# A fused two-layer perceiver block: masks, series and projections moved to where engines wait

## The chip, the cores and the metric

The kernel runs on one core of one Trainium2 chip. The metric is the device time of one execution of the whole program, in microseconds (us), lower is better. TensorE is called PE, VectorE DVE, ScalarE ACT, GpSimd POOL, and the queue of SyncE, from which the loads are issued, SP.

## The reference

Six residual sublayers work on x, 8 batches of 64 tokens of 512 numbers. Each takes the layer norm of x and adds its result to x.

```python
x = x + _L0_xattn_ref(_layernorm(x), ctx_2048, itok, ...)   # windowed latent attention over 9 context rows
x = x + _L0_attn_ref(_layernorm(x), ...)                    # differential attention
x = x + _L0_ffn_ref(_layernorm(x), w_gate_up, w_proj)       # ternary weights, silu(gate) * up, rms norm, projection
x = x + _L1_xattn_ref(_layernorm(x), ctx_2048, decay, W_in, b_in, W_out, b_out, gamma, beta)
x = x + _L1_attn_ref(_layernorm(x), ...)                    # int8 projections, rotary attention
x = x + _L1_ffn_ref(_layernorm(x), ...)                     # Hadamard transforms, 2048 hidden
...
good = (k_ids <= qs) & (k_ids >= qs - LOOKBACK)             # L0_xattn: 9 rows of 1601 per token, by its id
...
s = K * s + xt                                              # L1_xattn: x = kv W_in + b_in, K = sigmoid(decay)
summary = jnp.mean(states @ W_out.T + b_out, axis=1)        # one row per batch
```

Only the mean over the 1601 states of the fourth sublayer counts, so the kernel works with two weighted sums of the context rows per batch: the plain mean, and the sum weighted by a decay series of 1601 numbers.

## The kernel before, in words

One program in raw engine code: each engine has its own list of instructions, in the order in which the functions are called at the end of the file, and semaphores tie them. Nothing is scheduled; the order written is the order run. Most products are taken in three matmuls of fp32r parts (`mm3`, L41 to L43: high by high, low by high, high by low). A high part is a cast on ACT (`split_high`, L153, for weights), a low part a subtraction on POOL (`split_low`, L157) or DVE.

**Start of WindowAttention.** DVE makes the decay series as one scan of 1601 steps in one partition (`vector_series`, L324), sums it (`vector_total`, L329), turns the token ids into row numbers for the gathers (`ids`, L954 to L967), and then does the layer norm of x (L190 to L208, with PE turning xn and ACT taking the high part). PE spreads the series over partitions by 13 matmuls of one column (`tensor_columns`, L349 and L350). After the layer norm DVE takes the low parts of two weights (L1014), copies the group ids (L1016), and makes the masks of the windows (`group_masks`, `key_masks`: L974 to L997; `empty_windows`: L1003 to L1007). PE then makes the query latents `wa_qc` from W_dq (24 matmuls).

**Units of keys.** Four gathers (`wa_win`) bring 9 context rows for each of 128 tokens. They are worked off in 12 units u of three rows: PE turns (`turn`, L1173), ACT takes the high part (L855), DVE the low part (`keys_low`, L1029), PE compresses (`compress`, 12 matmuls), DVE copies to `wa_kst` (L1039), PE makes the rope keys (`rope_keys`, L1191). POOL rotates them (`rotate`, L770 to L775), PE turns the result (`rope_turn`, L1200), ACT copies it (`rope_out`, L847).

**Pairs of heads.** For 8 pairs i PE makes queries (L41 to L43, L1245), rope queries and `wa_qa`. ACT copies `wa_qn` high (L886), the sums of the pair before (`rotated`, four copies, L877), the rope keys, and then casts the weights of the next pair (L153), of which POOL takes the low parts (L157). PE begins pair i+1 when these are there.

**Rounds of attention.** 18 rounds of scores, softmax and context follow, with matmuls of the context sums among them until round 12.

**Seam to the ternary FFN and its rounds.** DiffAttention ends with x += (L1634); SP then issues loads, among them `ContextSummary.sync` (bias and two 1 MB weights); DVE, PE and ACT do the layer norm. PE makes 16 hidden tiles f, each a gate and an up product of 8 f16 matmuls (L2087). In the last two rounds it also does `tensor_state` (L410, L411: four groups of matmuls with 8 columns) and `tensor_summary` (L418, L419), both in one piece. ACT casts the projection weights `ff_wp` (L2030) after the last round; PE projects (L2101, L2102).

**Int8Attention.** ACT copies, takes exponentials and, between them, casts the first two weights of the last FFN (`ffn.high`, L2679); POOL takes their low parts (L2649). DVE scales y (L2369).

## Time and profile before

| what | value |
|---|---|
| median of 3 runs | 940.71 us (937.42 to 946.45) |
| profiled execution, its own time | 947.03 us |
| its span | 945.1 us |
| PE busy | 845.2 us (89%) |
| DVE busy | 617.8 us (65%) |
| ACT busy | 479.0 us (51%) |
| POOL busy | 167.9 us (18%) |
| mean granted clock of PE | 0.931 of full speed |

The span runs from the first to the last instruction; 1.9 us lie around it. The profiled execution is 6.3 us, or 0.7%, above the median of the three timed runs. Times in rows are counted from the start of the span.

### The profile page before, as it was taken

What the parts mean: (1) busy time and instruction counts of PE and PEld (TensorE: products, weight loads), DVE (VectorE), ACT (ScalarE), POOL (GpSimd) and SP (SyncE); (2) the same over time, 40 slices, a digit from 0 to 9 for tenths busy, and PEclk for the clock granted to TensorE, in tenths of its full rate; (3) what the DMA queues carried; (4) which work ended last, traced back from release to release, by engine and by line L of the source; (5) the groups of instructions that cost most, each with busy time, mean ns of one, the idle gap of its engine ahead of it and who ended that gap; (6) DMA issues with size and microseconds to landing.
All of it is one profiled execution on the core that took longest, in us unless ns stands there. A gap on an engine that the chain in (4) does not pass through costs nothing.

```text
span 945.1 us, 13986 instructions
## 1 busy us (share of the span) xinstructions
PE 845.2 (89%) x5323; PEld 638.2 (68%) x5323; DVE 617.8 (65%) x1056; ACT 479.0 (51%) x798; POOL 167.9 (18%) x168
## 2 busy tenths in 40 slices
PE   4899899999899798999999987998967666999997
PEld 4797555677778576887887874454743445888885
DVE  7654677567466658999999985433587877434233
ACT  2466675223275488777878643432335443434331
POOL 2044541000145410000000001331031112111112
PEclk9999999999589889999999999998988766999999
DMA  8633465761113544334443005004042610221201
GB/s 281 221 131 109 147 198 209 293 229 52 57 56 100 179 139 156 103 102 136 131 156 112 23 2 181 0 0 171 29 141 90 246 46 1 67 66 46 68 1 44
DMA packets 49628, 106.77 MB, mean 113 GB/s; under 512 B 6484, under 2 KB 25868, under 8 KB 45982
## 3 DMA queue, kind: packets, MB, share of 16 engines
q1 hardware_dynamic: 48670, 95.31, 30.3%
q0 software_dynamic: 896, 10.62, 2.9%
q8 instruction: 41, 0.67, 0.3%
q14 instruction: 21, 0.17, 0.1%
HBM read 100.67 MB, written 5.24 MB: 112 GB/s over the span
## 4 chain that ended last, share of the span: by engine, by line
PE 75%; DVE 12%; ACT 6%; issue 2%; POOL 1%; SPq 1%; DMA 1%; ACTq 0%; DVEq 0%; POOLq 0%
PE banks L41 15%; PE banks L43 14%; PE banks L42 14%; PE banks L2087 6%; PE banks L359 2%; PE banks L1339 2%; PE banks L2101 2%; PE banks L1309 2%; PE banks L2102 2%; PE banks L1710 2%; PE banks L1901 1%; PE banks L1312 1%; PE banks L1173 1%; PE banks L1191 1%; ACT tw_wide L1868 1%
## 5 line engine op out<-in xcount | busy, mean ns | idle before, releaser
L157 POOL TENSOR_TENSOR w_low<-w_raw,w_high 128x256 fp32r<-128x256 f32 (+2 forms) x44 | 58.2, 1332 | 175.0 <-ACT w_high L153 174.9
L153 ACT CAST w_high<-w_raw 128x1024 fp32r<-128x1024 f32 (+2 forms) x74 | 56.9, 780 | 23.8 <-PE banks L43 18.2
L41 PE MATMUL banks<-da_xT_high,w_high 128*128 128x512 f32 x128 | 52.6, 411 | 1.4 <-DVE da_xT_low L208 1.4
L41 PE MATMUL banks<-hf_xhh,w_high 128*128 128x512 f32 (+1 forms) x136 | 51.8, 381 | 0.4 <-DVE hf_xhl L2754 0.3
L43 PE MATMUL banks<-hf_xhh,w_low 128*128 128x512 f32 (+1 forms) x136 | 51.9, 382 | 0.0
L42 PE MATMUL banks<-hf_xhl,w_high 128*128 128x512 f32 (+1 forms) x136 | 51.8, 381 | 0.0
L2087 PE MATMUL banks<-ff_xT_high,tw_guT 128*128 128x512 f16 x128 | 49.8, 389 | 1.4 <-DVE ff_xT_low L208 1.4
L43 PE MATMUL banks<-da_xT_high,w_low 128*128 128x512 f32 x128 | 50.9, 398 | 0.0
L42 PE MATMUL banks<-da_xT_low,w_high 128*128 128x512 f32 x128 | 50.7, 396 | 0.0
L2087 PE MATMUL banks<-ff_xT_low,tw_guT 128*128 128x512 f16 x128 | 49.7, 388 | 0.0
L2670 POOL TENSOR_TENSOR hf_hl<-hf_h,hf_hh 128x512 fp32r<-128x512 f32 x16 | 24.3, 1519 | 124.7 <-ACT hf_hh L2726 124.7
L2734 DVE TENSOR_TENSOR hf_downW_l<-dw_w,hf_downW_h 128x512 fp32r<-128x512 f32 x16 | 11.2, 697 | 50.7 <-ACT hf_downW_h L2686 50.7
L1989 POOL MEMSET ff_acc<- 128x512 f32 x1 | 0.5, 530 | 239.9 <-DVE x_res L1634 239.9
L1578 DVE TENSOR_TENSOR w_low<-w_raw,w_high 128x1024 fp32r<-128x1024 f32 x28 | 33.7, 1224 | 6.6 <-ACT w_high L153 5.9
L41 PE MATMUL banks<-w_high,da_xT_high 128*128 128x256 f32 x128 | 37.1, 290 | 0.0
L43 PE MATMUL banks<-w_high,da_xT_low 128*128 128x256 f32 x128 | 36.2, 283 | 0.0
L42 PE MATMUL banks<-w_low,da_xT_high 128*128 128x256 f32 x128 | 36.1, 282 | 0.0
L2783 DVE TENSOR_TENSOR hf_downH_l<-banks,hf_downH_h 128x512 fp32r<-128x512 f32 x16 | 11.1, 692 | 35.0 <-ACT hf_downH_h L2722 35.0
L1868 ACT CAST tw_wide<-banks 128x1024 bf16<-128x1024 f32 x24 | 24.5, 1020 | 18.5 <-PE banks L1901 18.5
L912 ACT COPY wa_cn<-banks 72x512 f32<-72x512 f32 x16 | 9.3, 582 | 48.2 <-PE banks L1320 48.2
L2049 DVE TENSOR_TENSOR ff_e<-ff_e,banks 128x512 f32<-128x512 f32 x16 | 11.0, 688 | 34.1 <-PE banks L2087 34.1
L2716 ACT ACTIVATE hf_silu<-banks,hf_scales 128x512 f32<-128x512 f32 x16 | 11.0, 690 | 43.2 <-PE banks L43 43.2
(433 smaller groups left out, 2523.4 us busy)
## 6 DMA issues: line engine op xcount, KB each, us to landing
cs_rows<-in_ctx SPq DMA_DIRECT2D x24, 1024.0 KB, 5.0
tw_raw<-in_L_ffn_w_gate_up SPq DMA_DIRECT2D x16, 512.0 KB, 4.4
hf_raw<-in_L_ffn_W_up SPq DMA_DIRECT2D x16, 512.0 KB, 3.6
w_raw<-in_L_xattn_W_o SPq DMA_DIRECT2D x8, 512.0 KB
w_raw<-in_L_attn_Wq SPq DMA_DIRECT2D x8, 512.0 KB
w_raw<-in_L_attn_Wk SPq DMA_DIRECT2D x8, 512.0 KB
w_raw<-in_L_attn_Wv SPq DMA_DIRECT2D x8, 512.0 KB
w_raw<-in_L_attn_Wo SPq DMA_DIRECT2D x8, 512.0 KB
```

The source lines that it names most:

```text
L41: nc.tensor.matmul(out, a[0], b[0], start=start, stop=False)
L42: nc.tensor.matmul(out, a[0], b[1], start=False, stop=False)
L43: return nc.tensor.matmul(out, a[1], b[0], start=False, stop=stop)
L153: self.nc.scalar.copy(self.wh[k][:, 0:cols], self.raw[k][:, 0:cols]).then_inc(self.split_hi[k], 1)
L157: self.nc.gpsimd.tensor_tensor(self.wl[k][:, 0:cols], self.raw[k][:, 0:cols], self.wh[k][:, 0:cols].bitcast(F32), ALU.subtract).then_inc(s ...
L359: ins = nc.tensor.matmul(c.bank[32 * r:32 * r + 32, bank, :], self.col[:, k * self.R4 + r, :], self.rows[k][:, r, :], start=(k == 0), stop ...
L1309: nc.tensor.matmul(out[a], queries(self.qa, 8 * g), keys(self.kvcT[:, g // 16, g % 16, :, :]), start=True, stop=False)
L1339: ins = nc.tensor.matmul(c.bank[:, 6 + r % 2, q * P:(q + 1) * P], self.cn[(r - 2) % 3][:, q, :], self.pt[r % 2][:, q, :], start=True, stop ...
L1578: v.tensor_tensor(c.wl[k][:, :], c.raw[k][:, :], c.wh[k][:, :].bitcast(F32), ALU.subtract).then_inc(c.split_lo[k], 1)
L1868: self.c.nc.scalar.copy(self.wide[s % self.DEEP][:, :].rearrange("p (a n) -> p a n", a=2), self.c.bank[:, bank:bank + 2, :]).then_inc(self ...
L2087: ins = nc.tensor.matmul(c.bank[:, 2 * k + n, :], w.guT[:, j, bass.ds(i * 2 * P + k * P + n * F0, P)], part[:, j, :], start=(j == 0 and pa ...
L2670: g.tensor_tensor(self.hp[1][t % 2][:, :], self.h[t % 2][:, :], self.hp[0][t % 2][:, :].bitcast(F32), ALU.subtract).then_inc(self.hl_ok, 1)
```

## The change

What it does, by places:

- **Start.** The ids and their base load first on SP, before x. `ids` runs first on DVE, then the series; the total of the series, the ids of groups and all masks leave the start. The low part of W_dq is taken inside the layer norm (`ahead`), ahead of `xT_low`. The layer norm turns over four banks in place of two. PE's 13 matmuls of the series are gone: SP writes the series to DRAM and reads it back as columns (`sync_columns`), DVE scales them.
- **Units.** The six pieces lie after the copy to `wa_kst` of units 0 to 5 on DVE. The group ids' matmul is after unit 1 on PE. `rope_turn(6)` moves from the last unit to behind it, into one row with 7 and 8; banks of two rope turns change.
- **Pairs.** ACT casts the next weights ahead of `rotated`. POOL's first three `low` stand behind both halves of the last rotation.
- **Seam and FFN.** `ContextSummary.sync` is issued when the ternary weights are done, before DiffAttention ends. `tensor_state` is cut into four: two right after the first x +=, two in tiles 1 and 2; `tensor_summary` into four in tiles 4 to 7; its bias is added on DVE. The first gate and up products are done in halves of 256 tokens, the first when two of four `xT_low` are there. Four of eight rounds are written out, the rest stay a loop. ACT casts `ff_wp` 0 and 1 after its first round. `load_second` of the down weights is issued once the summary is done.
- **Int8Attention.** Both `ffn.high` come between the first exponentials and `turned(3)`.

```diff
@@ LayerNorm.vector_rest
                                     ALU.subtract, ALU.mult).then_inc(c.ln_xn, 1)
+        if ahead:
+            ahead(dve)
         if self.transposed:
@@ ContextSums
+    def sync_columns(self, sp):
+        sp.wait_ge(self.geo_ok, 1)
+        sp.dma_start(self.series, self.geo).then_inc(self.col_done, 16)
+        sp.wait_ge(self.col_done, 16)
+        sp.dma_start(self.col_in[:, 0:self.R], ...).then_inc(self.col_done, 16)
+            sp.dma_start(self.col_in[0:self.rest, self.R:self.R + 1], ...).then_inc(self.col_done, 16)
-    def tensor_columns(self, pe, at):
@@ ContextSummary
+    def tensor_state(self, pe, j):
+        if j == 0:
+            pe.wait_ge(cs.mean_ready, B)
...
+            pe.wait_ge(self.in_, 16 * 4)
+    def tensor_summary(self, pe, k):
+        if k == 0:
+            pe.wait_ge(self.cs.s_out, 1)
@@ WindowAttention.gpsimd
-            rotate(m, 0)
-            if m == M - 1:
-                low(0, 1)
-                low(1, 1)
-            rotate(m, 1)
+            for a in range(2):
+                rotate(m, a)
+        low(0, 1)
+        low(1, 1)
+        c.split_low(pool, 2, f[2] + 3, 2 * LAT)
@@ WindowAttention.scalar
+            if i < PAIRS - 1:
+                act.wait_ge(self.qr_done, i + 1)
+                high(0, i + 1)
+                high(1, i + 1)
             if i:
                 rotated(i - 1)
             if i in (1, 2, 3):
                 rope_out(8 + i)
-            if i < PAIRS - 1:
-                act.wait_ge(self.qr_done, i + 1)
-                high(0, i + 1)
-                high(1, i + 1)
@@ WindowAttention.vector, after the copy to wa_kst of unit u
+            if u == 0:
+                self.segments(dve, ch)
+            if u == 1:
+                self.cs.vector_total(dve, ch)
+            if u == 2:
+                self.group_masks(dve, ch)
+            if u == 3:
+                ch.wait()
+                self.cs.vector_columns(dve)
+                self.key_masks(dve, ch)
+            if u == 4:
+                self.key_offsets(dve, ch)
+            if u == 5:
+                self.empty_windows(dve, ch)
@@ WindowAttention.tensor
-            if u == self.UNITS - 1:
-                rope_turn(u - 5)
...
-        rope_turn(7)
-        rope_turn(8)
+            if u == 1:
+                pe.wait_ge(self.seg_f, 1)
+                nc.tensor.matmul(c.bank[:, 7, 0:self.G], self.rep[:, :], self.seg8f[:, 1, :], ...).then_inc(self.g_done, 1)
+        for u in (6, 7, 8):
+            rope_turn(u)
@@ TernaryFFN
+        round_(0, True)
+        projection(0)
+        projection(1)
...
+        def among(f):
+            if f in (1, 2):
+                self.cy.tensor_state(pe, f + 1)
+            if 4 <= f < 4 + C:
+                self.cy.tensor_summary(pe, f - 4)
+        early, late = slice(0, 2 * P), slice(2 * P, N)
+        pe.wait_ge(c.ln_lo, M * self.ln.t + 2)
+        for n in range(2):
+            product(0, n, early)
+        pe.wait_ge(c.ln_lo, M * self.ln.t + M)
@@ Int8Attention.scalar
         exponentials(0)
+        for t in range(2):
+            self.ffn.high(act, t)
         turned(3)
         probabilities(0)
         exponentials(1)
-        self.ffn.high(act, 0)
@@ build
+                window.sync_ids(sp)
                 sp.dma_start(core.ident[:, :], dram["ident"]).then_inc(core.const_in, 16)
...
+                sp.wait_ge(ternary.q_ok, ternary.STEPS)
+                ffn0.cy.sync(sp)
                 after_diff(sp)
...
+                pe.wait_ge(diff.y_add, 1)
+                for j in range(2):
+                    ffn0.cy.tensor_state(pe, j)
                 after_diff(pe)
```

On DVE, from the series to the first low part of the query latents, this stood before (`wa_segf`: ids as numbers, `wa_idx`: rows to gather, `wa_g`, `wa_vb`, `wa_vt`: masks):

```order
L324 SCALAR_TENSOR_TENSOR wa_kvcT<-cs_decay,cs_ones 1x1601
L329 TENSOR_REDUCE cs_tot<-wa_kvcT 1x1
L963 CAST wa_idx<-wa_segf 128x4
L190 BN_STATS ln_stats<-x_res 128x6 x4
L208 TENSOR_TENSOR wa_xT_low<-banks,wa_xT_high 128x4x128 x4
L1014 TENSOR_TENSOR w_low<-w_raw,w_high 128x1024
L1016 COPY wa_g<-banks 128x64
L992 TENSOR_TENSOR wa_vb<-wa_jrow,wa_g 128x576
L997 TENSOR_SCALAR wa_vb<-wa_vt 128x576
L1023 TENSOR_TENSOR wa_qcl<-banks,wa_qch 128x512
L1003 CAST wa_segs<-wa_segb 128x512
```

And this stands there now, on the same engine, up to the first units (rows between are left out in both):

```order
L980 CAST wa_idx<-wa_segf 128x4
L337 SCALAR_TENSOR_TENSOR wa_krT<-cs_decay,cs_ones 1x1601
L190 BN_STATS ln_stats<-x_res 128x6 x4
L1037 TENSOR_TENSOR w_low<-w_raw,w_high 128x1024
L210 TENSOR_TENSOR wa_xT_low<-banks,wa_xT_high 128x4x128 x4
L1037 TENSOR_TENSOR w_low<-w_raw,w_high 128x512
L1045 TENSOR_TENSOR wa_qcl<-banks,wa_qch 128x512 x2
L1049 TENSOR_TENSOR wa_cT_even_l<-banks,wa_cT_even_h 128x4x128 x3
L1059 COPY wa_kst<-banks 128x384
L985 CAST wa_seg8f<-wa_seg 8x64
L342 TENSOR_REDUCE cs_tot<-wa_krT 1x1
```

The low part of W_dq is ahead of `xT_low`, and nothing but the other weight's low part lies between `xT_low` and the query latents. The masks are among the units.

On ACT, in pair 1 of the heads, before (`wa_qnh`: queries high, `wa_qr`: rope queries, `w_high0` to `w_high2`: weights of the next pair):

```order
L886 CAST wa_qnh1<-banks 128x512
L877 COPY wa_qr<-wa_t10 64x256 x4
L847 COPY wa_krT<-banks 64x16x8 x3
L153 CAST w_high0<-w_raw 128x384
L153 CAST w_high1<-w_raw 128x256
L898 COPY wa_qa<-banks 128x512
L153 CAST w_high2<-w_raw 128x256
```

The same pair now:

```order
L904 CAST wa_qnh1<-banks 128x512
L153 CAST w_high0<-w_raw 128x384
L153 CAST w_high1<-w_raw 128x256
L895 COPY wa_qr<-wa_t10 64x256 x4
L866 COPY wa_krT<-banks 64x16x8 x3
L916 COPY wa_qa<-banks 128x512
L153 CAST w_high2<-w_raw 128x256
```

The two casts have passed the four copies of `wa_qr` and the rope keys.

On PE, between the last product of DiffAttention and the first hidden tile, the layer norm's turns stood alone before; now:

```order
L43 MATMUL banks<-w_high3,da_ol1 128x512
L418 MATMUL banks<-cs_mu,cy_wT0 128x8 x4
L419 MATMUL banks<-cs_tot,cy_bias0 128x8
L418 MATMUL banks<-cs_mu,cy_wT0 128x8 x4
L419 MATMUL banks<-cs_tot,cy_bias0 128x8
L243 MATMUL banks<-ident,ff_xn 128x128 x16
L2116 MATMUL banks<-ff_xT_high,tw_guT 128x256
L2116 MATMUL banks<-ff_xT_low,tw_guT 128x256
```

Two of the four groups of `tensor_state` stand at the seam, and the first products are halves.

## Rows read from the trace of the kernel before

**Rows 1.** The page: busy time of engines, and the chain that ended last.

```profile
PE 845.2 (89%) x5323; PEld 638.2 (68%) x5323; DVE 617.8 (65%) x1056; ACT 479.0 (51%) x798; POOL 167.9 (18%) x168
...
PE 75%; DVE 12%; ACT 6%; issue 2%; POOL 1%; SPq 1%; DMA 1%; ACTq 0%; DVEq 0%; POOLq 0%
```

**Rows 2.** Timeline, 0 to 36: start, duration, engine, line; in brackets idle before, releaser.

```profile
6.91 1.81 DVE L329 TENSOR_REDUCE cs_tot<-wa_kvcT 1x1 f32<-1x1601 f32 x1
...
11.08 2.45 DVE L190 BATCH_NORM_STATS2 ln_stats<-x_res 128x6 f32<-128x512 f32 x4
...
15.24 1.11 PE L241 MATMUL banks<-ident,wa_xn 128*128 128x128 f32 x4 [0.81 <-DVE wa_xn L203]
...
20.44 0.69 DVE L208 TENSOR_TENSOR wa_xT_low<-banks,wa_xT_high 128x512 fp32r<-128x512 f32 x1 [0.16 <-ACT wa_xT_high L231]
...
23.15 0.77 PE L41 MATMUL banks<-wa_xT_high,w_high 128*128 128x512 f32 x1 [3.36 <-DVE wa_g L1016]
...
31.89 0.43 DVE L1003 CAST wa_segs<-wa_segb 128x512 f32<-128x512 int32 x1 [2.67 <-DMA wa_cs<-in_q_sin]
...
35.96 0.44 PE L41 MATMUL banks<-wa_cT_even_h,w_high 128*128 128x384 f32 x1 [0.54 <-DVE wa_cT_even_l L1029]
```

**Rows 3.** Timeline: a low part of the units on DVE, the last unit on PE.

```profile
40.94 1.29 DVE L1029 TENSOR_TENSOR wa_cT_even_l<-banks,wa_cT_even_h 128x512 fp32r<-128x512 f32 x2 [2.04 <-ACT wa_cT_even_h L855]
...
83.87 0.52 PE L1200 MATMUL banks<-ident,wa_kr 128*64 128x128 f32 x3 [1.43 <-POOL wa_kr L775]
```

**Rows 4.** Waits of PE, whole span: total us, times, longest; then timeline, 99 to 105.

```profile
PE banks L41 <- POOL w_low L157: 4.4, 4, 2.3
...
99.65 2.60 ACT L877 COPY wa_qr<-wa_t 64x256 f32<-64x256 f32 x4 [0.21 <-POOL wa_t L806]
...
104.32 0.50 PE L41 MATMUL banks<-wa_qch,w_high 128*128 128x512 f32 x1 [2.30 <-POOL w_low L157]
```

**Rows 5.** Windows: length, busy of PE, PEld, DVE, ACT, POOL, granted clock, DMA, GB/s.

```profile
104.00:108.00 4.00, 3.68 (x13) 2.10 (x13) 0.83 (x1) 0.64 (x2) 2.89 (x4) 0.67 0.30 86
160.00:234.00 74.00, 73.06 (x602) 52.57 (x601) 48.55 (x133) 24.24 (x47) 0.73 (x1) 1.00 0.58 211
234.00:262.00 28.00, 23.44 (x112) 20.61 (x112) 15.33 (x39) 9.26 (x15) 3.08 (x2) 0.52 0.14 48
635.00:641.10 6.10, 6.10 (x20) 3.57 (x21) 0.47 (x2) 0.00 (x0) 0.00 (x0) 0.50 0.00 0
651.00:655.20 4.20, 3.53 (x9) 2.82 (x10) 2.75 (x4) 1.14 (x3) 1.27 (x1) 0.59 0.97 348
```

**Rows 6.** Timeline, the seam to the ternary FFN on PE.

```profile
576.06 3.34 PE L241 MATMUL banks<-ident,ff_xn 128*128 128x128 f32 x16 [3.38 <-DVE ff_xn L203]
...
580.79 0.39 PE L2087 MATMUL banks<-ff_xT_high,tw_guT 128*128 128x512 f16 x1 [1.40 <-DVE ff_xT_low L208]
```

**Rows 7.** Timeline, 630 to 652, PE: state, summary, first projection.

```profile
630.88 0.95 PE L410 MATMUL banks<-cs_mu,cy_wT 128*128 128x8 f32 x8
...
637.19 0.61 PE L2087 MATMUL banks<-ff_xT_high,tw_guT 128*128 128x512 f16 x1
...
642.73 3.60 PE L418 MATMUL banks<-cy_wT,cy_stateT 128*8 128x512 f32 x8
...
651.67 0.80 PE L2101 MATMUL banks<-ff_wp,ff_hh 128*128 128x512 f32 x1 [2.55 <-ACT ff_wp L2030]
```

**Rows 8.** Timeline, Int8Attention: an ACT copy, POOL's low part, DVE's scaling twice.

```profile
748.35 0.69 ACT L2232 COPY w_raw<-banks 128x640 f32<-128x640 f32 x1 [2.66 <-PE banks L2452]
...
752.68 2.42 POOL L2649 TENSOR_TENSOR w_low<-hf_raw,w_high 128x1024 fp32r<-128x1024 f32 x1 [22.64 <-ACT w_high L2679]
...
753.56 1.82 DVE L2369 TENSOR_SCALAR ia_y<-ia_y,ia_y_scale 128x512 f32<-128x512 f32 x1
...
756.75 1.51 PE L2498 MATMUL banks<-ia_v,ia_aT 64*64 64x33 f32 x64 [2.98 <-ACT ia_aT L2245]
...
769.07 0.48 DVE L2369 TENSOR_SCALAR ia_y<-ia_y,ia_y_scale 128x512 f32<-128x512 f32 x1
```

217 lines of the change are left out of this document (113 added, 104 removed).

## The prediction, made before the changed kernel was run

> **What bounds the kernel now.** The page comes first, for the busy shares and the chain that ended last. PE is busy for 89% of the span and carries 75% of that chain; DVE has 12% of it, ACT 6% [rows 1]. So the work on PE is the floor, and this change takes hardly any of it away: time can come from the places where PE stands idle, and from stretches in which PE works at a low granted clock. I looked for both. The waits of PE by what ended them and the timeline of PE, with what DVE, ACT and POOL did just before, give the idle places; the windows give the clock. The reader is to see in them that most of the waits are short, that the longest lie where a helper engine has a queue of other work in front of the one thing PE needs, and that two clock dips follow late stretches of narrow or interrupted PE work. The attention rounds, the longest part, are full at clock 1.00 over 160 to 234 [rows 5] and are not touched. The sum is made against the profiled execution's own time, 947.03 us; the median of the runs is 6.3 us below it, and I take that off at the end.
>
> **Start: 5.9 us (4.2 to 7.3).** The first compress of PE starts at 35.96. On DVE the series' sum, 1.81, stands ahead of the layer norm's statistics at 11.08 [rows 2]; it leaves for the units, so with the ids still ahead they start at about 9.3, and the first turn at 13.4 in place of 15.24. From first turn to last low part the layer norm takes 5.9 here (15.24 to 20.44 + 0.69 = 21.13) [rows 2], while the larger one at the seam takes 4.7 (576.06 to 580.79) [rows 6]; with four banks I take 4.7 here as well: ready at 18.1. PE's product then started at 23.15, behind the weight's low part and the copy of the group ids, which PE waited 3.36 for [rows 2]. Both are gone from there, so it starts at about 18.5: 4.65 us. After it, the mask of empty windows waited 2.67 on DVE for a load, with the second low part of the query latents behind it [rows 2]; I take half, 1.3, since PE had half of that stretch filled. The lower end is that the constants land no earlier and the statistics stay at 11.08 (less 1.7), the upper that the whole 2.67 comes back. The gathers now follow the ids directly and PE wants them only after the queries; SP's trip of the series through DRAM is wanted by nobody before the context sums.
>
> **Units: 0.2 us (-1.0 to 1.0).** PE's wait of 1.43 before the rope turn of unit 6 goes with the move of `rope_turn(6)`, but the turn itself comes later in one row with two others; I count 0.7. The group ids' matmul on PE costs up to 0.4. The masks now lie on DVE between low parts of keys. The idle slot there is 2.04 a unit [rows 3], and the one piece that has a row, the sum of the series, is 1.81 [rows 2], so each piece about fills its slot; I take 0.1 for what spills over. If each of six spilled 0.2, the term would be -1.0. If the slots covered all and the turn were hidden, it would be 1.0.
>
> There is a row that speaks against this placing. A scaling of `ia_y` on DVE took 1.82 with POOL's low part running beside it from 752.68, and 0.48 without such company [rows 8]. POOL rotates rope keys beside the units, and the key masks of unit 3 on DVE fall on that. The Trainium skill, GPSIMD Engine Reference, section 1 (Specifications), says that the engine's SBUF interfaces are shared with VectorE, with contention when DVE works in a 2-port mode or reads two SBUF inputs. The trace agrees for the scaling (0.48 against 1.82); by it, the masks, some of which read two tiles, would spill more. By the rows, I let it stand in the lower bound, because the rotation covers one unit out of six.
>
> **Pairs: 4.6 us (1.5 to 6.5).** PE waits four times for POOL's low part of a weight, 4.4 in all, the longest 2.30 at 104.32 [rows 4]. The cast on ACT that POOL needs stands behind four copies of 2.60 together, which start at 99.65 [rows 4]; now it stands ahead of them. After that longest wait the granted clock over 104 to 108 is 0.67 [rows 5]; its 4 us did the work of 2.7, so 1.3 more is lost there. 5.7 is there to be had. A quarter of the waits, 1.1, I keep back, since ACT is nearly full in these pairs and now brings the rotated queries and `wa_qa` 0.5 to 1 us later, which PE wants too: 4.6. POOL's first three low parts behind the last rotation have the rest of that unit as cover. At the low end ACT becomes the bound and returns only the clock and a little; at the top nothing is given back and the lost share of the clock is larger.
>
> **Seam: 0.9 us (-0.9 to 1.7).** PE stood idle 3.38 before the layer norm's turns and 1.40 before the first gate product [rows 6]. Two of four state groups, some 2.6 us by half of the 6.3 below less the slow clock, go into the first gap, nearly covered; the half product starts when two low parts of four are there, so most of the 1.40 can be used. I count 0.9, since the extra matmuls of halved products and the turns that now start behind state groups cost some. The low bound is that the 2 MB of weights land late: SP issues them some 10 us before they are wanted.
>
> **State out of the last rounds: 3.7 us (3.0 to 4.0).** The four groups run from 630.88 to 637.19, 6.3 us with no product beside them [rows 7]. Two remain in PE's stream, in tiles 1 and 2, at 1.3 each: 2.6.
>
> **Half clock behind it: 2.0 us (0 to 2.0).** From 635 to 641.1 the granted clock is 0.50, with PE busy for all of the 6.10 [rows 5]. What ran just before was the row of matmuls with 8 columns. About 2 of the 3 us lost there fall on ordinary products, which I expect at full clock once the narrow ones are spread out. That is a reading, not a proof, so 0 is the lower end. The Trainium skill, TensorE: Matmul & The Clock Gate, Part 1 (The HAM clock gate), says that the clock is set by how busy PE has been recently; the trace agrees only in part, with 0.50 over a stretch in which PE's records have no gap, and by the page alone I would count 0 here.
>
> **Summary: 0.4 us (-0.8 to 1.4).** Its eight wide matmuls are 3.60 of PE at 642.73 [rows 7] and stay; the bias matmuls go (about 1.4), and three more entries and exits among the products cost up to 1.
>
> **Wait for `ff_wp`: 2.55 us (2.0 to 2.6),** at 651.67, on ACT's cast [rows 7]. The cast moves to after the first round, 60 us ahead. Next late would be POOL's part, wanted only after the following tile: covered. **Half clock around it: 1.5 us (0 to 1.7).** From 651 to 655.2 it is 0.59 [rows 5], a loss of 1.7; without the wait ahead I take 1.5 back.
>
> **Heads of Int8Attention: 2.1 us (0 to 3.0).** ACT stands idle 2.66 before 748.35, and both of `ffn.high` go there. POOL's low part, which waits for them [rows 8], then runs earlier and no longer beside DVE's scaling at 753.56: 1.82 - 0.48 = 1.34. The cast no longer stands in the way of the next outputs, about 0.8. PE's idle 2.98 before 756.75 [rows 8] is the end of that chain and can take both.
>
> **Sum.** 5.9 + 0.2 + 4.6 + 0.9 + 3.7 + 2.0 + 0.4 + 2.55 + 1.5 + 2.1 = 23.85. From 947.03 that leaves 923.2, and 6.3 less is 916.9. I predict 917 us, 2.5% faster; with the smaller bounds partly met, 912 to 922.
>
> **The rivals.**
>
> *New waits take the place of the old (927, 922 to 932).* ACT, moved first, becomes late with `rotated` and `wa_qa`, and the pairs give 1.5 (3.1 less); both clock dips stay, because something else than the narrow matmuls and the wait makes them (3.5 less); the masks spill by 1.0 (1.2 less); the heads wait for PE's turns instead (2.1 less). Together 9.9 less. For it: ACT's load in the pairs, and the 0.50 with PE fully busy. Against it: each wait removed has a named cause with another piece of work ahead of it in the queue, and these are gone.
>
> *Loads are late (933, 930 to 938).* The change then does not do at the start and seam what it says: the ids' small load holds up the constants, the gathers or weights land after PE wants them, and the start gives 1.5 rather than 5.9, the seam -0.9. That is 6.2 beyond the case above. Against it: from the ids to the first turn of context rows there are some 18 us.
>
> *More (909).* The terms reach towards their upper ends: start 1.4, pairs 1.9, seam 0.8, summary 1.0, heads 0.9, units 0.8, and a little more.
>
> *Slower (953).* The clock, not the waits: over 234 to 262 the granted clock is 0.52, against 1.00 over the 74 us before [rows 5]. If the changed order ahead of the attention rounds left PE at the half level for their whole first stretch, 160 to 234, the cost, by the row at 0.52, would be 0.48 for each us spent in it. 75 us more of such a dip cost 36, and 917 becomes 953. It decides from 50 us of new half clock on, which eat the whole gain. Against it: nothing in that stage is changed.
>
> **How the numbers follow.** Chances: forecast 0.56, new waits 0.27, more 0.08, late loads 0.05, slower 0.04. The likeliest gives 917. From 908 to 931 the range takes in the forecast, the smaller gain and nearly all of the larger, and leaves out late loads, the slower case and the tails, under 2 in 10. One per cent, down to 931.3, is about what a measurement of this kernel can tell from no change. Faster by over 1%: the first three cases less a small tail, 0.90; within 1%: 0.06; slower: 0.04.
>
> **What the profile after would show.** The span near 921. First compress near 30. The waits of PE on POOL's low part of a weight together below 1.5, and no new waits of a us on ACT's copies in the pairs. No PE wait of a us in the last unit; idle slots of DVE in units 0 to 5 gone, with the unit's period the same. A granted clock near 1 where the rounds of the ternary FFN end and at its first projection, with no wait for `ff_wp`. The scaling of `ia_y` in the first head at 0.48. I am wrong if the two clock dips are still there, if ACT's copies stand as the enders of PE's waits, or if a product of the start waits for a load.

## The result and the profile after

The changed kernel takes 912.79 us in the median of 4 runs (910.99 to 913.76), the kernel before beside it 939.07 (935.98 to 946.45). The ratio is 0.9714, 95% interval 0.9678 to 0.9749. I had predicted 917 with 908 to 931 as the range. The profiled execution took 912.06 us, with a span of 910.0. Ratios leave out executions over 1.5% longer than the fastest of their kernel: none in these eight, three of 56 of the kernel before in the experiments.

The page of the changed kernel, busy time of the engines and the chain that ended last:

```profile
PE 815.7 (90%) x5298; PEld 621.0 (68%) x5311; DVE 614.0 (67%) x1056; ACT 480.3 (53%) x798; POOL 171.6 (19%) x168
...
PE 78%; DVE 14%; ACT 5%; issue 2%; DMA 0%; POOL 0%; SPq 0%; ACTq 0%; DVEq 0%
```

PE is busy for 29.5 us less than in [rows 1], although hardly any of its work went: many matmuls that ran at half clock there run at full clock here (mean granted clock 0.950 against 0.931). A part of that belongs to the one execution that [rows 1] show, as the first experiment says.

The timelines of DVE and PE at the start, to be read against [rows 2]: start, duration, engine, line; in brackets the idle time before, and what ended it.

```profile
9.66 2.43 DVE L190 BATCH_NORM_STATS2 ln_stats<-x_res 128x6 f32<-128x512 f32 x4
```

```profile
13.90 3.65 PE L243 MATMUL banks<-ident,wa_xn 128*128 128x128 f32 x16 [13.90 <-DVE wa_xn L203]
...
18.95 0.50 PE L41 MATMUL banks<-wa_xT_high,w_high 128*128 128x512 f32 x1 [1.40 <-DVE wa_xT_low L210]
...
23.88 0.39 PE L41 MATMUL banks<-wa_xT_high,w_high 128*128 128x512 f32 x1
...
28.64 0.44 PE L41 MATMUL banks<-wa_cT_even_h,w_high 128*128 128x384 f32 x1 [0.54 <-DVE wa_cT_even_l L1049]
```

The statistics start 1.4 earlier, the product of the query latents at 18.95 in place of 23.15, and the first compress at 28.64 in place of 35.96. Of these 7.3 us, 1.7 lie inside the product: it takes 4.93 from its first L41 to its last, where before it took 6.66 (23.15 to 29.81), the first matmul of it 0.50 against the 0.77 of [rows 2]. The next seven took 0.63 each before and 0.39 to 0.40 now. The windows show a granted clock of 1.00 over this product in both, so it is from the matmuls' own times that I call those of 0.63 half clock: matmuls of this shape take 0.63 in the changed kernel at 238 to 242, where the granted clock is 0.50.

The waits of PE in the stretch of the pairs, 80 to 160, in the changed kernel:

```profile
PE banks L41 <- issue: 1.0, 1, 1.0
PE banks L1341 <- DVE wa_qa L1109: 0.6, 1, 0.6
PE banks L41 <- ACT wa_kr_odd L859: 0.5, 1, 0.5
PE banks L41 <- DVE wa_t L1097: 0.4, 1, 0.4
```

The wait on POOL's low parts, 4.4 in [rows 4], is not there any more. What came in its place are 0.6 us ahead of the first scores and 0.4 ahead of another product. ACT is busy for 46.17 of the 60.60 us of that stretch, and it never ended a wait of PE on a pair's weights.

The seam on PE, against [rows 6]:

```profile
549.81 1.03 PE L418 MATMUL banks<-cs_mu,cy_wT 128*128 128x8 f32 x8 [0.29 <-DMA cy_wT<-in_L_xattn_W_out]
550.77 0.38 PE L419 MATMUL banks<-cs_tot,cy_bias 1*128 1x8 f32 x2
551.09 1.06 PE L418 MATMUL banks<-cs_mu,cy_wT 128*128 128x8 f32 x8
...
552.90 3.15 PE L243 MATMUL banks<-ident,ff_xn 128*128 128x128 f32 x16 [0.44 <-DVE ff_xn L203]
555.84 0.42 PE L2116 MATMUL banks<-ff_xT_high,tw_guT 128*128 128x256 f16 x1
```

Two groups of the state fill the gap of 3.38 down to 0.44, and the gap of 1.40 ahead of the first gate product is gone. The weights had landed but for 0.29.

Where [rows 7] had a wait of 2.55, the first projection follows directly, and the windows show no dip there (length, busy time of PE, PEld, DVE, ACT, POOL, granted clock, share of DMA, GB/s):

```profile
618.11 0.59 PE L2159 MATMUL banks<-ff_wp,ff_hh 128*128 128x512 f32 x1
```

```profile
614.00:618.00 4.00, 4.00 (x20) 1.83 (x19) 1.29 (x2) 1.33 (x4) 0.96 (x1) 1.00 0.00 0
618.00:622.00 4.00, 4.00 (x19) 3.01 (x16) 2.35 (x3) 2.06 (x4) 2.68 (x2) 1.00 0.52 172
622.00:626.00 4.00, 4.00 (x22) 3.35 (x22) 0.16 (x1) 1.42 (x3) 0.07 (x1) 1.00 0.99 363
```

### The profile page after: what moved, and what is told of

Same layout as the page of the kernel before. It is cut to its first block, busy times and chain, and to the rows that moved or that the text cites. A ratio compares the mean times of both kernels' runs of the same rounds, so it can differ in the third digit from the quotient of the medians.

```text
span 910.0 us, 13910 instructions
## 1 busy us (share of the span) xinstructions
PE 815.7 (90%) x5298; PEld 621.0 (68%) x5311; DVE 614.0 (67%) x1056; ACT 480.3 (53%) x798; POOL 171.6 (19%) x168
## 4 chain that ended last, share of the span: by engine, by line
PE 78%; DVE 14%; ACT 5%; issue 2%; DMA 0%; POOL 0%; SPq 0%; ACTq 0%; DVEq 0%
PE banks L41 16%; PE banks L43 15%; PE banks L42 15%; PE banks L2131 6%; PE banks L364 2%; PE banks L2159 2%; PE banks L1341 2%; PE banks L2160 2%; PE banks L1742 2%; PE banks L1371 1%; PE banks L1202 1%; PE banks L1344 1%; PE banks L1933 1%; ACT tw_wide L1900 1%; PE banks L243 1%
## 5 line engine op out<-in xcount | busy, mean ns | idle before, releaser
L41 PE MATMUL banks<-da_xT_high,w_high 128*128 128x512 f32 x128 | 52.5, 410 | 1.4 <-DVE da_xT_low L210 1.4
L41 PE MATMUL banks<-hf_xhh,w_high 128*128 128x512 f32 (+1 forms) x136 | 52.3, 385 | 0.2 <-DVE hf_xhl L2812 0.2
L2131 PE MATMUL banks<-ff_xT_high,tw_guT 128*128 128x512 f16 x120 | 45.5, 380 | 0.0
L2131 PE MATMUL banks<-ff_xT_low,tw_guT 128*128 128x512 f16 x120 | 45.5, 379 | 0.0
L41 PE MATMUL banks<-w_high,da_xT_high 128*128 128x256 f32 x128 | 37.1, 290 | 0.0
```

Source lines behind the costliest of these rows:

```text
L41: nc.tensor.matmul(out, a[0], b[0], start=start, stop=False)
L2131: ins = nc.tensor.matmul(c.bank[:, 2 * k + n, :], w.guT[:, j, bass.ds(i * 2 * P + k * P + n * F0, P)], part[:, j, :], start=(j == 0 and pa ...
```

## The experiments

Twelve experiments follow. The kernel before, run beside them, took 938.1 to 939.7 in the median.

To read them I cut each trace at the same eight places on PE and take the lengths between: the first compress, the first product of the pairs, the first scores, the first product of the output behind the attention rounds, the first gate product, the first projection, the first turn of Int8Attention, the first product of the last FFN, and the end of the span. "Before" is the profile that the prediction had, "again" the second one of the same kernel; the last column is the median of the timed runs. One stretch can differ by 1 us or more between two profiles of the same code in it, by where the clock is low.

| kernel | start | units | pairs | rounds | to gate | tiles | projection to Int8 | Int8 | rest | span | median |
|---|---|---|---|---|---|---|---|---|---|---|---|
| before | 35.96 | 53.17 | 68.19 | 109.08 | 314.39 | 70.88 | 64.60 | 79.58 | 149.25 | 945.1 | 939.07 |
| again | 35.61 | 53.16 | 67.05 | 100.90 | 315.17 | 70.83 | 64.60 | 79.63 | 149.15 | 936.1 | 938.43 |
| changed | 28.64 | 52.65 | 60.59 | 100.86 | 313.10 | 62.27 | 63.46 | 78.22 | 150.21 | 910.0 | 912.79 |
| ACT's order undone | 28.13 | 52.64 | 66.78 | 101.29 | 312.99 | 62.41 | 63.42 | 77.66 | 149.18 | 914.5 | 916.81 |
| state at the end | 30.03 | 52.65 | 60.91 | 100.82 | 313.04 | 66.09 | 63.10 | 78.22 | 150.24 | 915.1 | 916.24 |
| casts late | 27.77 | 52.64 | 60.54 | 101.22 | 313.79 | 64.74 | 64.40 | 77.86 | 149.54 | 912.5 | 915.01 |
| state in a row | 29.91 | 52.64 | 60.56 | 100.81 | 314.25 | 66.11 | 63.46 | 78.34 | 149.32 | 915.4 | 915.30 |
| `ffn.high` undone | 28.02 | 52.63 | 61.04 | 101.17 | 313.22 | 61.83 | 63.29 | 79.87 | 149.23 | 910.3 | 913.06 |
| masks in front | 41.64 | 52.32 | 61.57 | 100.90 | 314.64 | 61.77 | 63.34 | 78.13 | 149.69 | 924.0 | 924.55 |
| two banks | 32.27 | 52.64 | 61.58 | 101.09 | 314.19 | 61.77 | 63.59 | 78.64 | 149.53 | 915.3 | 914.57 |
| ACT's order alone | 36.02 | 53.20 | 60.51 | 100.76 | 314.32 | 72.49 | 63.03 | 79.70 | 149.27 | 929.3 | 931.41 |
| masks in a lump | 28.32 | 61.36 | 61.54 | 100.60 | 313.17 | 62.50 | 63.41 | 77.19 | 149.21 | 917.3 | 920.24 |
| fillers in five waits | 28.18 | 52.65 | 60.72 | 101.02 | 314.08 | 61.77 | 63.21 | 74.88 | 149.79 | 906.3 | 911.94 |
| fillers in Int8 | 30.17 | 52.64 | 60.62 | 100.61 | 314.90 | 61.77 | 63.39 | 74.29 | 148.01 | 906.4 | 911.21 |

**The kernel before, profiled again.** No edit.

> The kernel before, profiled once more. In its first profile the granted clock is 0.50 to 0.59 from 234 to 264, in the attention rounds behind the last context sum; the changed kernel has 1.00 in the same rounds, which makes 8.7 us of the 35 us between the two profiled spans. Theory A (the dip is a state that some executions have, not a part of the change): the new profile, or some of the timed runs, shows no such dip; span 935 to 940 with a mean clock near 0.95, and over all runs the time falls as the mean clock rises. Theory B (the dip belongs to the program of before, and the change removed it): the dip starts again within a few us of 234, span 944 to 947, mean clock 0.93.

Theory A. The span is 936.1, the rounds 100.90. The windows of the second profile and those of the first, in the same part of the attention rounds (columns as above):

```profile
236.00:242.00 6.00, 6.00 (x55) 5.63 (x55) 5.46 (x17) 2.07 (x4) 0.20 (x1) 1.00 0.30 105
```

```profile
242.00:250.00 8.00, 8.00 (x40) 7.26 (x40) 3.70 (x11) 1.47 (x3) 0.00 (x0) 0.50 0.01 2
250.00:262.00 12.00, 7.44 (x31) 6.09 (x31) 5.79 (x13) 5.32 (x8) 2.34 (x1) 0.50 0.17 55
```

PE does 55 matmuls in 6 us in the second profile, and 40 in 8 us in the first. The second has the half level only at the end of the rounds, 0.53 over 246 to 257, as the changed kernel has (0.50 over 236 to 240). Of the 35.1 us between the spans of the first profile and of the changed kernel, 8.2 us are a long half clock that this one execution had, and 1.1 the dip of [rows 5] behind the wait at 104, which the second profile does not have either (its wait of 2.3 is the same). Both do have another dip, further on in the pairs. In the second profile it is this:

```profile
151.00:154.00 3.00, 3.00 (x10) 1.86 (x14) 2.88 (x7) 2.56 (x4) 0.00 (x0) 0.50 0.01 5
```

The changed kernel has 1.00 throughout its pairs. Of 56 further executions of this kernel, 51 have a mean clock of 0.942 to 0.951 at 934 to 942 us, two 0.935 and 0.939 at 946 and 942, and three 0.930 to 0.932 at 949 to 951; the profile that the prediction was made from, with 0.931, belongs with these. Against the undisturbed one the change is worth 936.1 - 910.0 = 26.1 us, as the medians say.

**ACT's order in the pairs undone.**

```diff
             if i < PAIRS - 1:
-                act.wait_ge(self.qr_done, i + 1)
-                high(0, i + 1)
-                high(1, i + 1)
...
             if i in (1, 2, 3):
                 rope_out(8 + i)
+            if i < PAIRS - 1:
+                act.wait_ge(self.qr_done, i + 1)
+                high(0, i + 1)
+                high(1, i + 1)
```

> The changed kernel with one thing undone: ACT copies the rotated queries and the rope keys ahead of the casts of the next weights, as before. Theory A (the order on ACT made the whole gain of the pairs): PE's waits on POOL's low parts come back, 4 to 5 us in all, with a clock dip behind the longest, and the pairs end 6 to 7 us later: 919 to 920. Theory B (POOL's order or the earlier start of the pairs shares in it): 2 to 4 us later, 915 to 917, the waits on POOL shorter than the 4.4 of before and no dip.

In the stretch it is theory A: 66.78 against 60.59, 6.2 us, with the waits back, but no dip behind the longest. PE's longest waits from 80 to 160 in this kernel, and the clock around the wait of 2.1:

```profile
PE banks L41 <- POOL w_low L157: 4.5, 4, 2.1
```

```profile
92.00:96.00 4.00, 1.95 (x10) 1.28 (x9) 3.84 (x6) 3.92 (x10) 1.40 (x2) 1.00 0.00 1
96.00:100.00 4.00, 4.00 (x19) 2.27 (x18) 1.62 (x3) 1.73 (x4) 2.24 (x3) 1.00 0.40 115
```

The later dip is there again (0.57 over 143 to 147), and it counts in the 6.2. How much is seen in kernels that have ACT's new order: in the eight profiles without this dip the stretch is 60.5 to 61.0, in the three with it (masks in front, masks in a lump, two banks) 61.5 to 61.6. So about 1 of the 6.2 us is the dip, and 5.2 the order. The median, 916.81, is 4.0 above the changed kernel's, less than the stretch, and by its number it falls to theory B.

**ACT's order alone, in the kernel before.** The same lines, moved the other way in the old kernel.

> The kernel before with the one move on ACT alone: in the pairs, the two casts of the next weights ahead of the copies of the rotated queries and the rope keys. From the first product of the pairs to the first scores the undisturbed profile of before takes 67.05 us and the changed kernel 60.59, of which the kernel with this move undone gives back 6.2. Theory A (the move is worth that wherever it stands): 60.8 to 61.3 in that stretch, 932 to 933 in all. Theory B (it needs POOL's new order as well, since the low part waits behind the last rotations): 63 to 66, 935 to 938.

Theory A in the stretch, 60.51 against 67.05, of which again about 1 is the later dip, which this profile does not have. The median is 931.41, 6.8 below the kernel before, and the ratio 0.9941 (0.9916 to 0.9966). POOL's new order adds nothing that shows: the stretch is as short without it.

**State and summary back at the end.**

```diff
         def among(f):
-            if f in (1, 2):
-                self.cy.tensor_state(pe, f + 1)
-            if 4 <= f < 4 + C:
-                self.cy.tensor_summary(pe, f - 4)
+            if f == FT - 2:
+                for j in range(C):
+                    self.cy.tensor_state(pe, j)
+            if f == FT - 1:
+                for k in range(C):
+                    self.cy.tensor_summary(pe, k)
...
-                pe.wait_ge(diff.y_add, 1)
-                for j in range(2):
-                    ffn0.cy.tensor_state(pe, j)
```

> The changed kernel with the state and the summary put back into the last two rounds of the ternary FFN, the four groups of 8-column matmuls in one row (the bias of the summary stays on DVE). Theory A (narrow matmuls in a row pull the clock down): +4.3 for the matmuls and +2 to 3 for a half clock of some 5 us behind the row, in all 919 to 920. Theory B (the clock dip had another cause, such as the state of the throttle at that time): the matmuls alone, 916 to 917, with the granted clock at 1.00 behind the row.

The tiles take 3.8 us more, 66.09, and the median is 3.5 up. The four groups run from 608.13 to 613.3; the windows around them:

```profile
609.00:612.00 3.00, 3.00 (x24) 2.88 (x23) 0.00 (x0) 0.12 (x1) 0.97 (x1) 1.00 0.00 0
612.00:615.00 3.00, 3.00 (x16) 1.86 (x16) 0.19 (x1) 0.00 (x0) 0.00 (x0) 0.70 0.00 0
615.00:618.00 3.00, 3.00 (x12) 1.19 (x11) 1.16 (x2) 0.00 (x0) 0.00 (x0) 0.73 0.00 0
```

The dip is there, as theory A has it, and PE has no gap in it. It costs about (1 - 0.70 + 1 - 0.73) x 3 = 1.7 us; my 4.3 for the matmuls was too much, since two groups leave PE's stream at 1.3 each, 2.6. By the median alone, 916.24, theory B's number would have been met as well; it is the clock that speaks for A.

**All four groups in one row in tile 2.**

```diff
-            if f in (1, 2):
-                self.cy.tensor_state(pe, f + 1)
+            if f == 2:
+                for j in range(C):
+                    self.cy.tensor_state(pe, j)
```

> The changed kernel with all four groups of 8-column matmuls in one row in tile 2 of the ternary FFN, none at the seam; the summary stays in tiles 4 to 7. Theory A (a row of 36 narrow matmuls, 5 to 6 us at full clock, lets the clock fall): the granted clock drops to a half behind the row near 568 for some 5 us, the row and the dip cost 2.6 (the two groups that leave the gap at the seam) + 2 to 3: 917 to 918. Theory B (narrow matmuls do not matter to the clock): 1.00 behind the row, and 914.5 to 915.5.

The tiles take 66.11, the same as at the end of the rounds, and the dip comes with the row, 41 us earlier in the program:

```profile
568.00:572.00 4.00, 4.00 (x32) 3.88 (x31) 0.00 (x0) 0.78 (x2) 0.61 (x1) 0.98 0.00 0
572.00:576.00 4.00, 4.00 (x13) 1.48 (x14) 0.40 (x1) 0.00 (x0) 0.00 (x0) 0.60 0.00 0
576.00:580.00 4.00, 4.00 (x20) 1.84 (x19) 2.10 (x5) 1.85 (x4) 1.04 (x1) 1.00 0.00 0
```

Theory A for the clock: a row of 20 matmuls of 8 columns (40 in PE's records), 566.85 to 572.1, and then 1.7 us lost at half clock, wherever it stands. Both profiles of the kernel before and that of ACT's order alone have a dip that begins inside this row and lasts beyond it (in the last, 0.57 over 619 to 627). So it stands in five profiles of five with the row in one piece. Single groups between products show none (1.00 from 558 to 580 in the changed kernel). At the seam the clock is low for some us with two groups there (0.74 and 0.69 over 552 to 558) and without (0.53 over 555 to 558 in the kernel above), so nothing can be read from it on this. The median of 915.30 is 2.5 above the changed kernel and lies in theory B's range: the cost in the timed runs is smaller than theory A said.

**Casts of `ff_wp` late.**

```diff
         round_(0, True)
-        projection(0)
-        projection(1)
...
         for f in range(FT):
             if f >= 2:
                 act.wait_ge(self.y_done, f - 1)
-                projection(f)
+            projection(f)
```

> The changed kernel with the first two casts of the projection's weights on ACT put back behind all rounds. Theory A (the wait is the cause of the clock dip behind it): PE waits 2.5 us at the first projection, the granted clock falls to a half for 3 to 4 us behind it, together 4 us: 916 to 917. Theory B (the dip came from the narrow and skinny matmuls ahead): the wait of 2.5 alone, no dip, 915.

Theory A by the trace. The wait, and the clock behind it, which fell though no row of narrow matmuls was near:

```profile
620.70 0.80 PE L2157 MATMUL banks<-ff_wp,ff_hh 128*128 128x512 f32 x1 [2.62 <-ACT ff_wp L2061]
```

```profile
620.00:624.00 4.00, 3.30 (x8) 2.69 (x9) 0.51 (x1) 1.17 (x3) 1.43 (x1) 0.57 0.97 352
624.00:628.00 4.00, 4.00 (x23) 3.40 (x23) 0.32 (x2) 1.24 (x2) 0.00 (x0) 1.00 0.75 285
```

By the trace, tiles and projection together are 3.4 longer; the median, 915.01, is 2.2 up, which is theory B's number. And the wait does not bring the dip each time. The kernel with ACT's order alone has the same wait, 2.55, ahead of 637.30, and no dip behind it:

```profile
637.00:641.00 4.00, 3.70 (x16) 3.02 (x17) 2.39 (x3) 1.39 (x3) 1.10 (x1) 1.00 1.00 375
```

Its stretch from the projection to Int8Attention is 63.03, as short as in any kernel without the wait (63.1 to 63.6). So the dip stands in three profiles of four with the wait and in none of ten without.

**Both `ffn.high` where they were.**

```diff
         exponentials(0)
-        for t in range(2):
-            self.ffn.high(act, t)
         turned(3)
         probabilities(0)
         exponentials(1)
+        self.ffn.high(act, 0)
...
         exponentials(2)
+        self.ffn.high(act, 1)
```

> The changed kernel with the two casts of the last FFN's weights put back where they were on ACT in Int8Attention. My prediction priced this part at 2.1; the two traces show only 0.6 between the first head and the last FFN. Theory A (2.1 was right and something else took 1.5 back): 2 us slower, 915. Theory B (PE waits for a chain that the cast was hardly part of): 0.3 to 0.9 slower, 913 to 914, with DVE's scaling of ia_y again at 1.8 beside POOL.

DVE's scaling in this kernel with POOL's low part beside it (717.23, 2.41 us), then in the changed kernel:

```profile
718.16 1.76 DVE L2427 TENSOR_SCALAR ia_y<-ia_y,ia_y_scale 128x512 f32<-128x512 f32 x1
```

```profile
718.82 0.49 DVE L2427 TENSOR_SCALAR ia_y<-ia_y,ia_y_scale 128x512 f32<-128x512 f32 x1
```

The stretch of Int8Attention is 79.87 against 78.22, 1.65 us, near theory A; the median moved by 0.3, as theory B had it. The old order takes 79.6 to 79.9 in four profiles, the new one 77.2 to 78.6 in the eight without fillers, so the gain in the traces is 1.0 to 2.7, 1.7 between the means. The timed runs show no difference.

**Masks in front.** All masks and the sum leave the units and stand ahead of the query latents' low parts; the ids of groups (`segments`) stand inside the layer norm.

```diff
-            if u == 0:
-                self.segments(dve, ch)
...
         self.weights_low(dve, 0, C * LAT)
+        self.cs.vector_total(dve, ch)
+        self.group_masks(dve, ch)
+        ch.wait()
+        self.key_masks(dve, ch)
+        self.key_offsets(dve, ch)
+        self.empty_windows(dve, ch)
...
-                window.ln.vector(dve, ch, lambda eng: window.weights_low(eng, 2, C * 2 * P))
+                window.ln.vector(dve, ch, lambda eng: (window.segments(eng, ch), window.weights_low(eng, 2, C * 2 * P)))
```

> The changed kernel with the masks, the sum of the series and the ids of groups taken out of the units and put ahead of the low parts of the query latents, in DVE's idle stretch near 20 to 26. Theory A (the start gained because DVE was relieved): about 8 us of masks do not fit into an idle stretch of 5.2 us, the first compress comes 3 to 4 us later, the units are 0 to 0.5 shorter: 915.5 to 917. Theory B (the stretch is wide enough, or PE has slack there): within 1 us of 912.8.

Both theories missed: 924.55, and the first compress at 41.64. The cause is neither of theirs. DVE stood for a load:

```profile
25.78 0.18 DVE L985 CAST wa_seg8f<-wa_seg 8x64 f32<-8x64 int32 x1 [11.28 <-DMA wa_bd<-in_own_token]
```

In the changed program the small loads of the masks follow two weights in the queue, and land at 25.8. Before, the ids of groups were there at 13.77, when PE used them. So with this order of the loads the masks cannot stand at the start, and the kernel says nothing on what DVE's relief alone was worth there. The units are 0.33 shorter without masks (52.32), which bounds what the masks cost there.

**Masks in a lump.**

```diff
-            if u == 1:
-                self.cs.vector_total(dve, ch)
-            if u == 2:
-                self.group_masks(dve, ch)
             if u == 3:
+                self.cs.vector_total(dve, ch)
+                self.group_masks(dve, ch)
                 ch.wait()
                 self.cs.vector_columns(dve)
                 self.key_masks(dve, ch)
-            if u == 4:
-                self.key_offsets(dve, ch)
-            if u == 5:
-                self.empty_windows(dve, ch)
+                self.key_offsets(dve, ch)
+                self.empty_windows(dve, ch)
```

> The changed kernel with the sum of the series and all masks in one lump on DVE behind unit 3, in place of one piece a unit. They are some 8.5 us of DVE together. Theory A (the pieces are free only because each fits the 2 us that DVE is idle in a unit): the next low part of keys comes 6 us late, PE waits 5 to 6.5 us for it once and the clock may fall behind that wait (up to 2 more): 918 to 921. Theory B (PE is far enough ahead or the low parts have slack): within 2 us of 912.8.

Theory A, and a little more than it said for the stretch: the units take 61.36, 8.7 longer, 7.5 by the median (920.24). PE waits 6.16 (the profile names no engine for it), the granted clock behind that wait is 0.50, and DVE itself then waits for ACT's next high part:

```profile
55.15 1.30 PE L1218 MATMUL banks<-wa_wkr,wa_kst 128*128 128x64 f32 x5 [6.16 <-issue]
```

```profile
55.00:60.00 5.00, 4.85 (x20) 4.77 (x21) 1.88 (x4) 3.05 (x10) 0.00 (x0) 0.50 0.02 5
```

```profile
58.17 0.69 DVE L1049 TENSOR_TENSOR wa_cT_even_l<-banks,wa_cT_even_h 128x512 fp32r<-128x512 f32 x1 [3.12 <-ACT wa_cT_even_h L874]
```

The lump is 8.2 us (44.57 to 52.79). One idle slot of 2 us covered a part of it and 6.16 came back as PE's wait; the other 2.5 of the 8.7 is what half clock over these 5 us costs.

**The first layer norm on two banks.**

```diff
-            self.ln = LayerNorm(core, self.to, banks=4)
+            self.ln = LayerNorm(core, self.to)
```

> The changed kernel with the first layer norm back on two banks. Theory A (the banks are worth what the timelines say, 5.05 from the first turn to the product against 5.9): 0.8 to 1.2 us later at the first product and no more, 913.6 to 914. Theory B (the gap between PE's turns, 0.6, and a longer wait ahead of the product put it at half speed, as in the kernel before, where its first matmuls took 0.63 against 0.39): 2.5 to 3 us, 915.3 to 916.

```profile
16.61 1.94 PE L243 MATMUL banks<-ident,wa_xn 128*128 128x128 f32 x8 [1.16 <-DVE wa_xT_low L210]
19.95 0.79 PE L41 MATMUL banks<-wa_xT_high,w_high 128*128 128x512 f32 x1 [1.40 <-DVE wa_xT_low L210]
20.54 0.63 PE L42 MATMUL banks<-wa_xT_low,w_high 128*128 128x512 f32 x1
```

From the first turn to the product it is 6.44 against 5.05, 1.4 us for the banks, and half of the product's matmuls take 0.63, so that it is 7.56 against 4.93. The first compress is 3.6 later, the median 1.8. With the wait between the turns (both profiles of before, this one, ACT's order alone) or a longer one ahead of the product (masks in front), the product was slow in this way, 6.7 to 7.6, in five profiles of five; with four banks in three of eight (6.8 to 7.0: the state at the end, the state in a row, fillers in Int8; the kernel with fillers at the start is left out), and it took 4.9 in the others. In masks in front the windows show 0.50 at it; in the other slow ones they show 1.00, and half clock is read from the 0.63 of the matmuls. So the shorter wait seems to make the full clock likely, not certain. By the trace the cost is theory B's; the median, 914.57, lies between the two theories.

**Fillers in five waits.** Matmuls that nobody reads, in waits of PE.

```diff
+def keep_warm(core, n, bank):
+    for _ in range(n):
+        core.nc.tensor.matmul(core.bank[:, bank, 0:P], core.identb[:, :], core.identb[:, :], start=True, stop=True)
...
+        keep_warm(c, 24, 5)
         pe.wait_ge(self.o_out, R)
         values(0, 0, 0)
...
+        keep_warm(c, 30, 0)
         for m in range(M):
             pe.wait_ge(self.xq_ok, m + 1)
```

> The changed kernel with matmuls whose result nobody reads, put into five waits of PE so that it stays busy in them: 70 at the start (around the turns of the layer norm), 36 at the end of the attention rounds, 30 ahead of the first turns of Int8Attention, 24 ahead of its rotated heads. The product of the query latents took 4.9 us at full clock in four profiles of kernels like the changed one and 6.8 to 7.1 at half clock in two; behind the attention rounds PE works at 0.50 for some 5 us, and at 0.50 from 681 to 690. Theory A (idle time of PE brings the clock down, and any matmul keeps it up): full clock at those four places, 2 to 2.5 us less behind the rounds, 2 to 3 at the start of Int8Attention, 907 to 910. Theory B (the clock does not follow small fillers, or the fillers delay the matmuls behind them by as much): 912 to 915.

**Fillers in Int8Attention alone.** The same in six waits there and in one at the last FFN's transform.

> The changed kernel with unread matmuls in the waits of Int8Attention and of the last FFN's first transform alone: 36 ahead of the first turns, 36 ahead of the rotated heads, 10, 30, 10 and 6 ahead of the four output projections, 30 ahead of the transform. In the kernel with fillers in five waits the stretch 681 to 690 was at 1.00 in place of 0.50, and from the first turn of Int8Attention to the first product of the last FFN it took 74.88 in place of 78.22, but its timed runs spread from 907 to 917, and the fillers at the start and behind the attention rounds brought nothing. Theory A (the gain is Int8Attention's and holds): 72 to 75 for that stretch, 907 to 910 in the median, with less spread. Theory B (execution to execution the clock falls elsewhere instead): stretch 75 to 78, median 911 to 913.

The stretch 680 to 690, in the changed kernel and with the fillers of the second kernel:

```profile
680.00:690.00 10.00, 6.98 (x31) 3.86 (x33) 3.53 (x8) 5.43 (x9) 1.15 (x4) 0.50 0.06 22
```

```profile
680.00:690.00 10.00, 6.68 (x70) 4.63 (x71) 5.95 (x14) 5.91 (x11) 0.38 (x2) 1.00 0.33 123
```

In Int8Attention theory A holds by the trace: the mean granted clock of the stage is 0.78 and 0.84 in place of 0.70, and it takes 74.9 and 74.3 in place of 78.2. Behind the attention rounds 36 fillers kept the clock up for a while (1.00 over 232 to 236 and 0.83 over 236 to 240, where the changed kernel has 0.57 and 0.50), but the product there came 0.6 later and ran mostly at the half level, and the rounds took 101.02, no less than before. At the start the product was at 4.9, as in five of eight kernels without fillers. In all, the medians are 911.94 (907 to 917) and 911.21 (908.4 to 912.1), with ratios of 0.9699 (0.9645 to 0.9753) and 0.9715 (0.9695 to 0.9735) to before; the changed kernel's is 0.9714. Neither is shown to beat it, and both medians are near or in theory B's ranges.

## Why the prediction held

By its own steps, against the undisturbed profile of before:

| term | predicted | measured | by |
|---|---|---|---|
| start | 5.9 | 7.0 | 35.61 to 28.64 |
| units | 0.2 | 0.5 | 53.16 to 52.65 |
| pairs | 4.6 | 6.5 | 67.05 to 60.59 |
| seam | 0.9 | 2.1 | 315.17 to 313.10 |
| state, half clock, summary, wait | 3.7 + 2.0 + 0.4 + 2.55 = 8.65 | 8.6 | 70.83 to 62.27 |
| half clock around the projection | 1.5 | 1.1 | 64.60 to 63.46 |
| heads | 2.1 | 1.4 | 79.63 to 78.22 |
| rest | 0 | -1.0 | rounds 0.04, end 149.15 to 150.21 |
| sum | 23.85 | 26.1 | |

**Start.** The steps came as told but for their sizes, read from the timelines, since of its parts only the banks could be judged by an experiment: statistics 1.3 earlier rather than 1.8, the layer norm 5.05 rather than 4.7, the product 4.1 earlier rather than 4.65, 0.6 for the stretch behind it rather than 1.3. The missing term is the time of the product itself, 7.21 to 4.93, 2.3 between these two profiles. The prediction did not have it; its upper end was made of a wait of DVE alone. That the total of 7.0 lies in the range is in part luck, as three of eight kernels with four banks have the slow product too.

**Units.** Right: no wait of a us in the last unit, and pieces that fit. What makes them free is the spread, shown by the lump at 8.7, of which 6.16 is PE's wait.

**Pairs.** The mechanism was right and the size off in two pieces that cancel in part. I counted 1.3 for a clock dip that only the first profile had, and kept 1.1 back for ACT, which took nothing. The undoing and the single move, 6.2 and 6.5, put nearly all of the term on ACT's order, the waits foremost (4.8 in the second profile). But about 1 of it is the dip late in the pairs, at 153 in the profile that the prediction had, which it did not look at. That dip stands in all three profiles with the old order and in three of eleven with the new one, so the order may have a part in it; this was not tried. Without it the gain is 5.5. The measured 6.5 stands at the upper end of the range, and it gets there by this dip.

**Seam.** The stretch of the table is 300 us long and holds much else: kernels with the same seam have 313.0 to 314.9 in it, kernels with the old one 314.3 to 315.2, so its 2.1, above the upper end of 1.7, is in part chance. Closer to the place, from the start of DiffAttention's last product to the first gate product, it is 8.0 to 8.6 in three profiles with the old seam and 6.5 to 7.2 in the nine with the new one, 1.3 between the medians. 0.9 was a little too careful. The state's groups were nearly free: without them at the seam that distance is 6.6 and 7.2.

**Tiles.** The sum is right to 0.1, and three kernels show parts of it: the state with its dip 3.8, the wait 2.5 with 0.9 more behind it. The other 2.3 of the 8.6 (the summary's bias, a dip that was longer in the old kernel) was not tried by itself. The narrow row as a cause of the dip, which I had called a reading and not a proof, is now shown at two places. The wait as the cause of the other dip is shown in part: removed, the dip is gone in all ten profiles, and put back, it returned once, but one kernel that kept the wait had no dip. The 1.1 of the projection is in that sense not in every execution either.

**Heads.** The scaling at 0.48 came (0.49). Of the 2.1 the traces show about 1.7, the runs nothing.

**The rivals.** New waits in place of the old did not come: neither ACT in the pairs nor the masks under the rotation. The rule of the Trainium skill, GPSIMD Engine Reference, section 1, that the engine's SBUF interfaces are shared with VectorE, with contention when DVE reads two SBUF inputs, would have put the masks' spill at more than I took. The rows of units 2 and 3 on DVE and of the rotation on POOL in the changed kernel:

```profile
42.04 0.81 DVE L1007 TENSOR_TENSOR wa_g<-wa_g 128x64 f32<-128x64 f32 x1
45.29 0.74 DVE L1014 TENSOR_TENSOR wa_vb<-wa_jrow,wa_g 128x576 f32<-128x576 f32 x1
```

```profile
44.50 0.79 POOL L788 TENSOR_TENSOR wa_kr<-wa_kr,wa_tab 128x288 f32<-128x288 f32 x1
45.24 2.14 POOL L789 TENSOR_TENSOR wa_kr<-wa_kr,wa_tab 128x288 f32<-128x288 f32 x1
```

The mask of unit 3 reads two inputs beside the rotation and is as fast as at the start of before (0.76); the product on POOL took 2.14 in place of 0.79. The last piece of unit 2, also with two inputs, did spill: 0.81 beside POOL's product at 41.97, against 0.22 in the lump, where POOL was done. The trace agrees that there is contention. It cost DVE 0.6 once and POOL 1.3 once, and PE waited for neither. Late loads: the two weights landed 0.29 late, and nothing else; that the small loads are late, at 25.8, is true, but in the program as it is nothing waits for them. The slower case has this much in it that the dip of the first profile, on which it rested, comes in some executions and not in others, and costs about 8 us. Whether the change has a part in it is open: of the 47 executions of the changed kernel and its variants none has a mean clock below 0.943, of the 56 of the kernel before five are at 0.939 or less, but nothing in the attention rounds was changed, and no experiment tried it.

**The total.** Taking the terms off the profiled execution's own time and then 6.3 for the median was right, and only just: some of that execution's surplus, the dip at 104, was counted as a gain of the change as well. Of the 4.1 us between 916.9 and 912.79, 2.4 are gain beyond the sum (26.3 between the medians against 23.85), and 1.6 came from the starting point: 940.71 was the median of three runs, and it is 939.07 with the fourth.

## What to carry to other kernels

An operation that moves among steps with idle slots is free only piece by piece: 8.2 us of masks cost at most 0.3 in six pieces, and 8.7 with its clock dip in one. Before a term is made of a clock dip, ask whether a second execution has it. Of the four dips in [rows 5] one was gone and one much shorter in the second profile of the same kernel; one, behind a row of narrow matmuls, stood wherever the row stood; and one, behind a wait, in three profiles of four. In a queue with several customers, look first for the short operation that a slow chain needs and that stands behind work with slack: two casts moved ahead of four copies gave 5 to 6 us.

## What the runs showed of the hardware

- Behind a row of 20 matmuls with 8 columns (40 records, 5.2 us), with no gap in PE's records, the granted clock was 0.60 over 4 us at one place of the program and 0.70 to 0.73 over 6 us at another. It was 1.00 behind single groups of five between wide matmuls.
- The scaling of 128x512 on DVE takes 0.49 alone and 1.76 to 2.29 beside POOL's low part; a mask product of DVE with two inputs, 128x576, takes 0.74 beside POOL's product, which then takes 2.14 against 0.79; a smaller one, 128x64, took 0.81 against 0.22, and POOL's product beside it 0.80.
- Fillers of 128 columns in bf16 in waits of 1 to 4 us of Int8Attention raised its mean granted clock from 0.70 to 0.78 and 0.84, and the stage took 3.3 and 3.9 us less. Behind the attention rounds they raised the clock as well, and the rounds took no less time.
- After a wait of 2.6 us ahead of the projection the granted clock was 0.57 over 4 us in one kernel, and after the same wait, 2.55, it was 1.00 in another.
- One program's executions differ in where the clock is low: 0.930 to 0.932 in the mean at 949 to 951 us, 0.942 to 0.951 at 934 to 942. Where it is low in the slowest is seen in one profile only, which has 0.52 over 234 to 262, where the other profile has 1.00 until about 246.
